# The opening of a batched graph-attention kernel: G first, then half of pair 0's V, then T for pairs 0 and 1 together

## The reference, cut to what matters

```python
# x: (32, 256, 512), adj: (32, 256, 256) int32, three 512 x 512 weights
output = einsum('bni,io->bno', x, weight)
q, k = einsum('bni,io->bno', x, wq), einsum('bni,io->bno', x, wk)
alpha = einsum('bno,bmo->bnm', q, k)
alpha = maximum(alpha, 0.0) * (adj != 0)
alpha = softmax(alpha, axis=1)
x = layernorm(x + einsum('bnm,bmo->bno', alpha, output), axis=-1)
```

## Time and profile before

| | us |
|---|---|
| median of 3 runs | 523.43 (523.17 to 524.75) |
| the profiled execution, its own time | 521.46 |
| its span, first to last instruction | 519.7 |
| TensorE busy | 512.3 |
| VectorE, ScalarE, GpSimd busy | 370.0, 326.9, 256.6 |

### The profile page before, as it was taken

How to read it: one execution, slowest core, us unless ns; L and a number is a source line. 1 busy time by engine, 2 the same in 40 slices (tenths; PEclk the granted TensorE clock), 3 DMA queues, 4 the chain that set the end, 5 groups by cost and what they waited for, 6 DMA issues and landing times.

```text
span 519.7 us, 9909 instructions
## 1 busy us (share of the span) xinstructions
PE 512.3 (99%) x3247; PEld 466.3 (90%) x3247; DVE 370.0 (71%) x743; ACT 326.9 (63%) x749; POOL 256.6 (49%) x197
## 2 busy tenths in 40 slices
PE   8999999999999999999999999999999999999995
PEld 6889898899989998899988999889998999889994
DVE  5766845776948677586866779577684867757586
ACT  5565566386763857639574586638676385764676
POOL 0397894339635377155661486333953537710011
PEclk9999999999999999999999999999999999999999
DMA  8404241044330616024250333404342061501425
GB/s 285 161 1 160 82 168 60 21 140 146 129 135 20 219 64 242 20 59 183 113 205 20 127 137 110 177 20 170 112 180 83 20 222 61 202 1 37 165 102 221
DMA packets 30879, 62.05 MB, mean 119 GB/s; under 512 B 2064, under 2 KB 3344, under 8 KB 30864
## 3 DMA queue, kind: packets, MB, share of 16 engines
q1 hardware_dynamic: 30576, 61.48, 32.9%
q10 hardware_dynamic: 288, 0.39, 0.2%
HBM read 45.09 MB, written 16.78 MB: 119 GB/s over the span
## 4 chain that ended last, share of the span: by engine, by line
PE 97%; DVE 2%; issue 0%; POOLq 0%; POOL 0%; DVEq 0%
PE o_bank L319 12%; PE o_bank L321 12%; PE o_bank L320 12%; PE chain L321 11%; PE chain L319 11%; PE chain L320 11%; PE bank_y L319 6%; PE bank_y L320 6%; PE bank_y L321 6%; PE bank_z L319 3%; PE bank_z L321 3%; PE bank_z L320 3%; PE o_bank L653 1%; PE chain L496 0%; PE chain L501 0%
## 5 line engine op out<-in xcount | busy, mean ns | idle before, releaser
L1445 POOL TENSOR_TENSOR s_lo<-xs,s_hi 128x512 fp32r<-128x512 f32 x60 | 81.5, 1377 | 34.9 <-ACT s_hi L695 34.9
L1440 POOL TENSOR_TENSOR a_lo<-xt,a_hi 128x512 fp32r<-128x512 f32 x42 | 58.3, 1396 | 61.5 <-ACT a_hi L687 61.5
L321 PE MATMUL o_bank<-t_hi,a_lo 128*128 128x256 f32 x256 | 72.5, 283 | 0.0
L320 PE MATMUL o_bank<-t_lo,a_hi 128*128 128x256 f32 x256 | 72.5, 283 | 0.0
L319 PE MATMUL o_bank<-t_hi,a_hi 128*128 128x256 f32 x256 | 72.4, 283 | 0.0
L1436 POOL TENSOR_TENSOR xs<-xt 128x512 f32<-128x512 f32 x30 | 39.1, 1317 | 47.0 <-DMA xt<-in_x_t 30.2
L1450 POOL TENSOR_TENSOR rstd<-var_eps,minus_half 128x4 f32<-128x4 f32 x14 | 14.2, 1018 | 92.7 <-DVE var_eps L1134 92.7
L714 ACT COPY parts<-chain 128x256 f32<-128x256 f32 x90 | 33.2, 369 | 40.3 <-PE chain L321 39.1
L320 PE MATMUL chain<-w_lo,s_hi 128*128 128x256 f32 x180 | 51.0, 283 | 0.0
L321 PE MATMUL chain<-w_hi,s_lo 128*128 128x256 f32 x180 | 51.0, 283 | 0.0
L319 PE MATMUL chain<-w_hi,s_hi 128*128 128x256 f32 x180 | 51.0, 283 | 0.0
(11 more groups left out here) (209 smaller groups left out, 1627.3 us busy)
## 6 DMA issues: line engine op xcount, KB each, us to landing
xt<-in_x_t SPq DMA_DIRECT2D x64, 256.0 KB, 3.1
xn<-in_x SPq DMA_DIRECT2D x16, 1024.0 KB, 5.3
out<-xn SPq DMA_DIRECT2D x14, 1024.0 KB, 6.0
adj<-in_adj_t SPq DMA_DIRECT2D x16, 512.0 KB, 6.0
xn<-in_wq_t SPq DMA_DIRECT2D x4, 256.0 KB, 5.6
parts<-in_wk_t SPq DMA_DIRECT2D x4, 256.0 KB, 5.7
out<-xn SPq DMA_DIRECT2D x2, 512.0 KB, 2.8
xn<-in_w SPq DMA_DIRECT2D x3, 256.0 KB, 5.0
```

The source lines that it names most:

```text
L320: nc.tensor.matmul(dst, a[0], b[1], start=False, stop=False, skip_group_check=shared)
L321: return nc.tensor.matmul(dst, a[1], b[0], start=False, stop=last, skip_group_check=shared)
L1440: nc.gpsimd.tensor_tensor(a_lo[:, slot, u], xt[:, u], a_hi[:, slot, u].bitcast(F32), ALU.subtract).then_inc(a_lo_ready[slot], 1)
L1445: nc.gpsimd.tensor_tensor(s_lo[:, slot, s], xs[:, s], s_hi[:, slot, s].bitcast(F32), ALU.subtract).then_inc(s_lo_ready[slot], 1)
```

## The change

TensorE now starts with G: three rows of it k by k as wq and wk arrive (hi·hi, then hi·lo, then lo·hi over the rows), then row 3 (now in `bank_y`). Rows 0 and 1 of pair 0's V follow, then T of pairs 0 and 1 together as seven products at 512 columns, V's row 2, pair 0's scores, V's row 3, pair 1's scores, pair 0's output, V of pair 1. T's second half of P2 goes to `o_bank[0]`. The extra copies of B12 in `p_hi` and `p_lo` and the plain T go away. The warm-up's seven matmuls become fourteen of half the width.

S1 to S4 are now made for pair 0 too. Half of the first pairs' splits move from GpSimd to VectorE: S3 and S2 of both pairs, A11 and A12 of pair 1; GpSimd keeps S1, S4, A22 and A21. Pair 1's blocks load at once, into `soft` and `parts` instead of `xt`. All queues are ordered anew, and the counts of the waits shift with them. The diff, cut to the orders and the new functions (removed lines only for the loads and TensorE's order; `split_first_s` and `split_first_b` are subtractions of 512 columns as those of `split_s` and `split_b`, `split_qk` and `split_x0` too):

```diff
+FIRST_A, FIRST_S = (A11, A12, A22, A21), (S3, S1, S2, S4)
+FIRST_LO = {S3: 1, S2: 2}, {S1: 1, S4: 2}
...
+        v0_bank = [bank_y[:, 0], bank_z[:], o_bank[0][:], o_bank[0][:]]
...
-                sp.dma_start(quarter(xt, k), x0_t[k].rearrange("q (b n) -> q b n", b=2)).then_inc(x0_loaded[k], 16)
+                sp.dma_start(wq_raw[:, k], wq_rows[:, k]).then_inc(wq_loaded[k], 16)
                 if k > 0:
-                    sp.dma_start(w_raw[:, k], w_rows[:, k]).then_inc(w_loaded[k], 16)
+                    sp.dma_start(wk_raw[:, k], wk_rows[:, k]).then_inc(wk_loaded[k], 16)
+            for u in range(4):
+                sp.dma_start(xt[:, u], x_t[0].rearrange("q (u k n) -> q u k n", u=4, k=2)[:, u]).then_inc(
+                    x0_loaded[u], 16)
             for k in range(K):
-                sp.dma_start(wq_raw[:, k], wq_rows[:, k]).then_inc(wq_loaded[k], 16)
-                sp.dma_start(wk_raw[:, k], wk_rows[:, k]).then_inc(wk_loaded[k], 16)
+                sp.dma_start(w_raw[:, k], w_rows[:, k]).then_inc(w_loaded[k], 16)
+            for u in (A11, A21, A12, A22):
+                sp.dma_start(x1_raw[u], x_t[1].rearrange("q (u k n) -> q u k n", u=4, k=2)[:, u]).then_inc(
+                    x1_loaded[u], 16)
+            sp.dma_start(adj[:], adj_t[0].rearrange("q (r n) -> q r n", r=R)).then_inc(adj_loaded, 16)
             sp.wait_ge(a_lo_ready[0], 4)
-            for u in range(4):
-                load_block(1, u)
-            sp.dma_start(adj[:], adj_t[0].rearrange("q (r n) -> q r n", r=R)).then_inc(adj_loaded, 16)
+            for u in (A11, A21, A22, A12):
+                sp.wait_ge(x_summed[0], READ_BY[u])
+                load_block(2, u)
             sp.wait_ge(gt_lo_ready, 4)
             load_xn(0, 0)
-            sp.wait_ge(x_summed[1], 4)
-            sp.wait_ge(a_lo_ready[1], 4)
-            for u in range(4):
-                load_block(2, u)
             load_adj(1)
...
+                both = slice(0, 2)
+                pe.wait_ge(g_lo_ready, 2)
+                pe.wait_ge(b_lo_ready, B_LO_FIRST[A11])
+                t_half(P1, 0, both)
+                t_half(P1, 1, both)
+                pe.wait_ge(g_lo_ready, 4)
+                pe.wait_ge(gt_summed, 1)
+                pe.wait_ge(b_lo_ready, B_LO_FIRST[A12])
+                pe.wait_ge(v_lo_ready, 2)
+                t_half(P2, 0, both)
+                t_half(P2, 1, both, o_bank[0][:])
+                pe.wait_ge(gt_lo_ready, G_ORDER.index(T3) + 1)
                 xs_split(S3)
+                t_half(P7, 0, both)
+                pe.wait_ge(gt_summed, 8)
+                t_half(P7, 1, both)
...
+            def fill_first_v(r):
+                if r == 0:
+                    pe.wait_ge(w_lo_ready, K)
+                    pe.wait_ge(a_lo_ready[0], 2)
+                if r == 2:
+                    pe.wait_ge(a_lo_ready[0], 4)
+                    pe.wait_ge(t_summed, 2)
+                if r == 3:
+                    pe.wait_ge(v_lo_ready, 3)
                 for k in range(K):
+                    left, right = v0_parts(r, k)
+                    last = add_chunk(v0_bank[r], left, right, k == 0, k == K - 1)
+                last.then_inc(v0_filled, 1)
...
+            def fill_first_o():
+                pe.wait_ge(v_lo_ready, R)
+                for r in range(R):
+                    if r % M == 0:
+                        pe.wait_ge(p_lo_ready, r + M)
+                    if r in (1, 2):
+                        pe.wait_ge(masked, 2 + r)
+                    if r == 3:
+                        pe.wait_ge(added, 1)
+                    fill_row(r, o_bank[r % 3][:])
...
-            for _ in range(7):
-                nc.tensor.matmul(o_bank[1][:], s_hi[:, 0, 0, 0, 0:P], s_hi[:, 0, 0], start=True, stop=True)
-            fill_first_v()
+            for _ in range(14):
+                nc.tensor.matmul(o_bank[1][:, 0], s_hi[:, 0, 0, 0, 0:P], s_hi[:, 0, 0, 0], start=True, stop=True)
             fill_g()
+            fill_first_v(0)
+            fill_first_v(1)
             fill_first_t()
-            fill_last_of_first_v()
-            pe.wait_ge(t_lo_ready, 4)
-            fill_scores(0, 0)
-            fill_scores(0, 1)
-            fill_second_t()
-            fill_o_b(0, first=True)
-            pe.wait_ge(t_lo_ready, 4 + T_LO[0][A12])
-            pe.wait_ge(added, 2)
-            fill_scores(1, 0)
-            pe.wait_ge(t_lo_ready, 8)
-            pe.wait_ge(added, 3)
-            fill_scores(1, 1)
+            fill_first_v(2)
+            fill_first_s()
+            fill_first_v(3)
+            fill_s_b(0)
+            fill_first_o()
             fill_v(1, 1, first=True)
...
+            split_wq(0)
+            for k in range(1, K):
+                split_wk(k)
+                split_wq(k)
+            split_x0(A11)
+            split_x0(A12)
             for k in range(K):
+                split_w(k)
+            split_first_a(A11)
+            split_first_s(0, S3)
+            split_g(0)
+            split_g(1)
+            split_first_a(A12)
+            split_g(2)
+            split_first_s(0, S1)
+            split_first_s(0, S2)
+            split_g(3)
+            split_first_s(1, S3)
+            split_gt(T3)
+            split_first_v(0)
+            split_gt(T2)
+            split_first_v(1)
+            split_first_s(0, S4)
+            split_first_s(1, S1)
+            split_first_s(1, S2)
+            copy_first_t(P1, 0)
+            copy_first_t(P1, 1)
...
+            split_first_v(2)
+            for b in W_ORDER[:-1]:
                 split_wt(b)
+            split_s(1, 0, S2, first=True)
+            split_s(1, 0, S3, first=True)
+            split_t_b(0, A11)
+            split_t_b(0, A12)
+            exponent(0, 0)
+            exponent(0, 1)
+            split_t_b(0, A21)
+            split_t_b(0, A22)
+            exponent(0, 2)
+            exponent(0, 3)
             for r in range(R):
+                split_p(0, r, first=True)
+            split_first_v(3)
+            split_s(1, 0, S1, first=True)
+            split_s(1, 0, S4, first=True)
             for u in (A21, A11, A12, A22):
                 split_a(1, 0, u, first=True)
+            split_wt(D4)
             exponent(1, 0)
...
+            split_qk(wq_lo, wq_raw, wq_hi, 0, 1)
+            for k in range(1, K):
+                split_qk(wk_lo, wk_raw, wk_hi, k, 2 * k)
+                split_qk(wq_lo, wq_raw, wq_hi, k, 2 * k + 1)
+            split_x0(1, A11)
+            split_x0(2, A12)
             for k in range(K):
+                dve.wait_ge(w_hi_ready, k + 1)
                 b = k // 2 * 2
                 rest(w_lo[:, b:b + 2, k % 2], w_raw[:, k].rearrange("q (j n) -> q j n", j=2),
                      w_hi[:, b:b + 2, k % 2]).then_inc(w_lo_ready, 1)
+            split_first_b(A11)
             dve.wait_ge(qk_lo_ready, 2 * K)
+            split_g(0)
+            sum_gt(T1, 0)
+            split_g(1)
+            sum_gt(T1, 1)
+            split_first_s(0, S3)
+            split_g(2)
+            sum_gt(T3, 0)
+            sum_gt(T2, 0)
+            split_first_b(A12)
+            split_g(3)
+            sum_gt(T3, 1)
+            sum_gt(T2, 1)
+            sum_gt(D4, 0)
+            sum_gt(D4, 1)
+            split_first_s(0, S2)
+            split_first_v(0)
+            split_gt(T3)
+            split_first_s(1, S3)
+            split_first_v(1)
+            split_gt(T2)
+            split_first_s(1, S2)
...
+            dve.wait_ge(x_summed[1], 4)
+            dve.wait_ge(a_lo_ready[1], 2)
+            mask(0, 0, first=True)
+            relu_max(0, 0)
+            relu_max(0, 1)
+            split_t_b(0, A11)
+            split_t_b(0, A12)
+            mask(0, 1, first=True)
+            relu_max(0, 2)
+            relu_max(0, 3)
+            split_t_b(0, A22)
+            split_t_b(0, A21)
             invert(0)
             split_p(0, 0)
             split_p(0, 1)
+            split_first_v(3)
             split_p(0, 2)
             split_p(0, 3)
+            mask(1, 0)
+            mask(1, 1)
+            for r in range(R):
+                relu_max(1, r)
+            for r in range(R):
+                residual(0, 0, 0, r)
             means(0, first=True)
...
+            sum_first_x(0, S3)
+            sum_first_x(0, S1)
+            sum_first_x(0, S2)
+            sum_first_x(1, S3)
+            split_first_s(0, S1)
+            sum_first_x(1, S1)
+            sum_first_x(0, S4)
+            sum_first_x(1, S2)
+            split_first_s(0, S4)
+            sum_first_x(1, S4)
+            split_first_s(1, S1)
+            split_first_s(1, S4)
+            split_first_a(A22)
+            split_first_a(A21)
+            pool.wait_ge(w_lo_ready, K)
...
             for s in (S3, S1, S2, S4):
                 sum_x(1, 0, s, first=True)
+            for b in W_ORDER[:-1]:
+                split_wt(b)
+            for s in (S2, S3, S1, S4):
+                split_s(1, 0, s)
             for u in (A21, A11, A12, A22):
```

(29 more changed lines are left out.)

444 lines of the change are left out of this document (198 added, 246 removed).

## The result

| | before | after |
|---|---|---|
| median (runs) | 522.95 us (6) | 528.4 us (6, 528.03 to 528.85) |
| ratio of the runs, 95% interval | | 1.0095 (1.0079 to 1.0111) |
| profiled execution, its span | 521.46, 519.7 | 528.53, 526.7 |

The change makes the kernel 5.45 us slower; 528.8 was forecast. The profiled execution of after lies on the median of its runs. So the traces differ by 7.0 us where the runs differ by 5.45, and it is the 7.0 that can be followed step by step.

A forecast was written before the change was run, and what follows sets the result against it. TensorE, busy 512.3 of 519.7 us, was taken as the bound. Terms -2.0 - 0.2 + 0.3 + 1.6 + 3.3 + 0.1 + 2.5 = +5.6, the walk +5.3; +5.4 taken on 523.43 gave 528.8 us, range 521.0 to 532.0.

The forecast's parts named there:

- V row 0, +1.6: Before V row 0: TensorE waits for VectorE's w_lo, delayed by three collisions with GpSimd's sums; +1.6 us (0 to 1.9).
- the +0.3 for wq's cast at k = 1: In G: wk is cast first, so wq's cast ends about 8.2 against TensorE's 7.9; +0.3 us (0 to 0.65).
- G's start: After the warm-up: G starts when the first loads are split, as V did (4.74); costed at nothing, bounds -0.25 and +0.3 us.
- P2, +3.3: T's P2: its first half waits for VectorE's split of V row 1, ending at 30.1 against TensorE's 26.8; +3.3 us.
- Rival 3, the clock, 0.08: Behind P2's hole: idling puts TensorE back to slow matmuls, 2.5 us more, 531.3 us in all; chance 0.08.
- V of pair 1, +2.5: Before V of pair 1: TensorE, there at 69.0, waits for GpSimd's last split of w's sums until 71.4; +2.5 us.
- 0.1 forecast: In the outputs: one output row may wait 0.1 us for its mask.
- Nothing for adj, x0's late splits, pair 3's blocks: Pair 1's adj just in time for its mask, two x0 splits before V row 2, pair 3's loads: all costed at nothing.
- T at 512 columns, -2.0: T of pairs 0 and 1 as 84 matmuls of 512 columns: 19.07 us instead of 10.88 + 10.19, 2.0 us less.
- the old hole, -0.2: Row 3 of pair 0's output: the wait for a bank at 58.70 to 58.92 us goes away, 0.2 us less.
- The walk: Four engine queues followed in the new order: V of pair 1 starts at 71.5 against 66.16, +5.3 us.

The follow-up runs named there:

- Kernel 3: Changed kernel with GpSimd's sums of pair 0 begun only when w is split: 529.85 us, ratio 1.0125 to before.
- Kernel 1: Changed kernel with V row 1 in an output bank instead of the one T's P2 needs, P2's wait for VectorE removed: 527.26 us.
- kernel 5: Changed kernel with V row 1 in an output bank and the last W sum split early: 525.82 us.
- kernel 6: As kernel 5, with the mask of pair 1's first half ahead of VectorE's last two P splits: 525.28 us.
- kernel 11: kernel 6 plus a GpSimd wait, P2's first half (not V row 1) in an output bank, V's high parts first, later V row 1 split, unread matmuls before P7: 524.11 us.
- kernel 4: Changed kernel with 13 matmuls nobody reads ahead of P2's wait, which stays: 527.31 us.
- kernel 2: Changed kernel with the cast and split of w's last sum (D4) moved ahead of six of pair 2's splits: 526.34 us.
- kernel 8: Changed kernel with matmuls nobody reads ahead of two waits that stay, nine at V row 0 and thirteen at P2: 526.94 us.

## Why the prediction was right, point by point

The direction, the mechanism and the size held; part of the size held by luck, because errors cancel in three places.

- *V row 0, +1.6.* 1.9 measured; w_lo ended at 18.49 against 18.65 worked out. TensorE was there sooner than forecast (16.7 against 17.1): the +0.3 for wq's cast at k = 1 did not come, and G's start at 4.61 was where V's had been, as bounded. Kernel 3 shows that the collisions are the cause.
- *P2, +3.3.* 3.3 measured, VectorE ending at 30.13 against 30.1, TensorE arriving at 27.0 against 26.8. Kernel 1 shows that this wait was the hole. That the end fits to 0.03 us is luck. The sum had VectorE without a pause from 12.3; in fact it began 0.4 earlier and then stood 1.3 us idle for ScalarE's cast of w. And its collisions cost 4.35 us by the distances of the starts (2.07 over w's four splits, 0.14 to 1.06 for each of four later ones), not 5.2: 1.08 was the price of the worst of them.
- *Rival 3, the clock, 0.08.* This is the step that failed. The forecast took the clock as staying up and priced its fall at 2.5 us; it did fall, for 1.7 us. I had priced it by the whole start and given it little, with no row in mid-kernel for it. A hint was there: the warm-up's slow matmuls came behind idling as well. The Trainium skill ("TensorE: Matmul & The Clock Gate", section "HAM oscillation — how this bites in real kernels") describes a kernel whose waits put TensorE back to half clock each time, so that the next matmuls start slow. The trace agrees: 3.25 us of idling, granted clock 0.54 behind it.
- *V of pair 1, +2.5.* 1.1 measured. GpSimd needed 18.9 us from the end of the first scores (54.2, its first mask) to the last w_lo (73.1), against 19.1 worked out. But output row 1 had already waited 0.8 for its mask, 0.1 forecast: two P splits took 2.98 us beside GpSimd, 0.88 for the pair ahead of them, a collision that I had not walked, since it is not a plain subtraction. What is late in one place is not late twice. So this term was too large and that one too small, and their sum is 0.7 us below the forecast.
- *Nothing for adj, x0's late splits, pair 3's blocks.* No wait of TensorE names them. Adj was issued at 59.1 and there well before the mask at 66.9, so it had more room than "just in time".
- *T at 512 columns, -2.0, and the old hole, -0.2.* The sum bears them out: waits 7.1, in starts of matmuls 7.7, the clock 1.7, less 2.2, makes 7.2 where V1 moved by 7.0. The holes of the forecast (0.3 included) were 7.8 in all: their sum is better than its parts.
- *The total.* The walk said 71.5 for V of pair 1; it was 73.2, 1.7 later, the clock. I took the shift to the median of before, as if the profiled execution of before were only faster by a constant. The runs differ by 5.45, the traces by 7.0, so the clock's 1.7 and the 1.5 by which before's profile beat its median cancel. What before's usual runs lose against its best was not profiled and stays open. The clock is a part of it in its slowest runs only: of 77 runs of before beside the experiments, the seven with a mean granted clock of 0.995 or less took 524.7 to 525.8 us, but those at 0.999 spread from 521.2 to 524.0.

Kernels 1, 5, 6 and 11 add what the prediction had not said: a hole repaid early in the opening is mostly spent again behind it. From the changed kernel to kernel 11 the scores come 4.9 us earlier and V1 4.5, but only after each of three later collisions or waits was dealt with by itself. VectorE and GpSimd are busy longer in the first 76 us than before the change (57.5 and 51.3 us against 49.5 and 48.8), in part because their steps stretch each other, and TensorE has 2 us less to hide it under.

## What to carry to other kernels

Before an order is made tighter for TensorE, add up what the engines that feed it must do up to each wait, with the price that a step has while its neighbour is busy, and not only the sum of durations: here queues with no slack cost 9.4 us (7.7 in holes, 1.7 by the clock) for 2.2 saved. Where a collision falls on the critical path and the other engine has slack, one wait on that engine is the cheap repair (1.5 us of idling there bought a hole of 1.7 back). And price a hole in TensorE of a few microseconds with the slow matmuls behind it.

## What the hardware showed that was not expected

- **The clock falls in mid-kernel, and not always at the same hole.** After idling of 2.0 and 2.2 us ahead of V row 0 the granted clock was 0.57 from 18 to 22 us (kernels 4 and 2), after 1.9 us in the changed kernel it stayed at 1.00 there and fell behind P2. The length of the hole alone does not decide it: ahead of output row 1 TensorE idled 1.80 us in kernel 1 and 1.81 in kernel 5, and only in kernel 5 was the clock low behind it (0.70 from 68 to 72 us). Some nine matmuls then started 0.43 us apart instead of 0.23, 1.7 us. Matmuls whose results nobody reads kept it up (kernel 8).
- **VectorE steps that read PSUM kept their time beside GpSimd, those that took both inputs from SBUF did not, in both operations seen here.** `t_lo` and `w_lo` subtractions took 1.1 to 1.8 us each instead of 0.69, and the P splits (scale, then subtract, 256 columns) 1.2 to 1.5 instead of 0.44; the `v_lo` from banks took 0.68 to 0.69.
